# A mixture-of-experts decoder layer: the last four experts on one of two sums, and the odd tiles' statistics by accumulating passes

## The reference

```python
probs = softmax(x @ router_weight.T); topw, topi = top_k(probs, 8)
topw = topw / sum(topw)
# each expert takes its rows, at most 256 of them (CAPACITY)
gu = xe @ gate_up_proj; g, u = split(gu, 2); h = silu(g) * u
ye = h @ down_proj
y = sum over the 8 experts of a row of topw * ye
x = x + y
out = (x - mean(x)) / sqrt(var(x) + 1e-5)     # over the 512 values of a row
```

## Time and profile before

| | |
|---|---|
| median of 3 runs | 1366.23 us (1363.86 to 1369.6) |
| the profiled execution | 1370.82 us |
| its span, first to last instruction | 1368.9 us |
| mean granted TensorE clock | 0.88 |
| busy: PE, DVE, ACT, POOL | 1144.9, 1100.1, 852.6, 997.2 us |
| HBM read and written | 147.48 and 52.94 MB |

### The profile page before, as it was taken

One profiled execution on the slowest core, in us unless ns is written; L12 is line 12 of the kernel. 1 busy time (PEld: TensorE's weight loads), 2 busy tenths in 40 slices (PEclk: granted clock), 3 DMA queues, 4 the chain that ended last, 5 costly groups with the idle time before them and its releaser, 6 DMA issues. The chain is left out here.

```text
span 1368.9 us, 19497 instructions
## 1 busy us (share of the span) xinstructions
PE 1144.9 (84%) x6481; PEld 768.9 (56%) x6481; DVE 1100.1 (80%) x1534; ACT 852.6 (62%) x1536; POOL 997.2 (73%) x788
## 2 busy tenths in 40 slices
PE   7489997898968889978987536999999999999950
PEld 2234433353324544333533326999899999999950
DVE  2379988989968699778899354988889888989946
ACT  5474584734855445756354225888888888888843
POOL 0778778867999887999989703777777777777744
PEclk9688997899979689977998557999999999999985
DMA  6535326322252412163131208999999999999978
GB/s 239 136 74 193 103 64 154 108 56 72 49 139 57 129 51 64 34 152 108 31 81 32 62 17 277 267 305 303 308 301 303 307 307 307 303 314 304 302 130 331
DMA packets 97491, 235.26 MB, mean 172 GB/s; under 512 B 20705, under 2 KB 21217, under 8 KB 96753
## 3 DMA queue, kind: packets, MB, share of 16 engines
q1 hardware_dynamic: 65648, 162.66, 39.1%
q0 software_dynamic: 31744, 71.37, 21.8%
HBM read 147.48 MB, written 52.94 MB: 146 GB/s over the span
## 5 line engine op out<-in xcount | busy, mean ns | idle before, releaser
L1189 DVE TENSOR_TENSOR_SCAN hst<-hst,dbu 128x512 f32<-128x512 f32 x256 | 299.2, 1214 | 98.8 <-POOL dbu L1005 72.9
L1005 POOL TENSOR_TENSOR dbu<-rep,bc 128x1024 f32<-128x1024 f32 x128 | 301.8, 2359 | 67.1 <-PE y_ps L377 36.1
L1600 POOL DMA_INDIRECT sum_rows<-ye,tokens x128 | 205.5, 1605 | 101.0 <-ACT ye L1679 73.9
L377 PE MATMUL y_ps<-dbu,cs 128*32 128x512 f32 x512 | 158.0, 701 | 74.7 <-DVE dbu L1195 63.5
L1592 POOL DMA_INDIRECT xe<-x_rows,tokens x128 | 148.9, 1163 | 83.6 <-issue 37.8
L771 ACT ACTIVATE hst<-rep,small_sb 128x512 f32<-128x512 f32 x256 | 165.9, 685 | 47.7 <-DVE dbu L1195 42.1
L415 PE MATMUL ring<-wqkv,xT 128*128 128x512 f32 x384 | 178.7, 609 | 0.3 <-DVE x2T L1277 0.2
L1195 DVE TENSOR_TENSOR dbu<-hst,bc 128x1024 f32<-128x1024 f32 x128 | 156.7, 1225 | 4.4
L1642 PE MATMUL low<-xh,w1h 128*128 128x256 f32 x512 | 150.8, 295 | 0.7 <-DVE w1l L1753 0.7
L1642 PE MATMUL low<-xl,w1h 128*128 128x256 f32 x512 | 145.6, 284 | 0.0
L1642 PE MATMUL low<-xh,w1l 128*128 128x256 f32 x512 | 145.5, 284 | 0.0
(11 more groups left out here) (190 smaller groups left out, 2705.6 us busy)
## 6 DMA issues: line engine op xcount, KB each, us to landing
w<-in_gate_up SPq DMA_DIRECT2D x64, 768.0 KB
rep<-made SPq DMA_DIRECT2D x256, 128.0 KB
w<-in_down SPq DMA_DIRECT2D x64, 256.0 KB
bc<-bc_rows SPq DMA_DIRECT2D x64, 128.0 KB, 2.9
w<-in_down SPq DMA_DIRECT2D x64, 128.0 KB
rows<-sum_rows SPq DMA_DIRECT2D x16, 512.0 KB, 9.3
sum_rows<-x2T SPq DMA_DIRECT2D x1, 4608.0 KB, 16.7
xT<-in_x_turned SPq DMA_DIRECT2D x16, 256.0 KB, 3.0
```

The source lines that it names most:

```text
L377: ins = pe.matmul(y_ps[rows, :], sel, dbu[:, n % WORK, g, :], start=(k == 0), stop=(k == QUADS - 1))
L1005: pool.tensor_tensor(dbu[:, n % WORK, :, :], rep[:, i % 2, :, 1, :], bc[:, k, 0, :].unsqueeze(1).broadcast_to([P, 2, T]), ALU.mult).then_i ...
L1189: dve.tensor_tensor_scan(h, h, dbu[:, n % WORK, i, :], 0.0, ALU.mult, ALU.add).then_inc(scanned, 1)
L1600: pool.indirect_dma_start(sum_dram[e % SUMS], bass.IndirectOffsetOnAxis(ap=tokens[:, e, j:j + 1], axis=0), ye[:, e % YE, j, :], None, comp ...
```

## The change

The last four experts, 60 to 63, all add to the even sum (`sum_of`), so the odd sum is complete with expert 59 (`ALONE - 1`). `scatter(e)` for 61, 62 and 63 waits for the expert right before it; up to 60 it waits for e-2 as before. SP loads the whole odd sum when 59 has landed, and the whole even sum when 63 has.

In the last stage the two tiles of a pair are treated differently. For the odd tile DVE adds the sums by `scalar_tensor_tensor`, which also writes the sum over each row (`total`). ACT turns that into minus the mean and makes a Square of the tile plus this bias, with the sum over each row as a further output (`power`). For the even tile DVE does what it did for every tile. POOL copies and scales the odd tile's two numbers beside the even tile's and then works on the pair as before. ACT does `center(g + 1)` ahead of the normalization of pair g.

```diff
--- before.py
+++ after.py
@@ -1466,8 +1466,7 @@
         YE = 3
         PER = 2
         PARTS = TILES // PER
-        LOADS = ((0, 0), (0, 1), (0, 2), (1, 0), (1, 1), (0, 3), (1, 2), (0, 4), (1, 3), (0, 5), (1, 4), (0, 6), (1, 5),
-                 (0, 7), (1, 6), (1, 7))
+        ALONE = EXPERTS - 4
         tab_i = sb("tab_i", [P, P], I32)
         tab_f = sb("tab_f", [P, P])
         last_f = sb("last_f", [P, P])
@@ -1491,8 +1490,11 @@
         twice_l = sb("twice_l", [P, 2, CAP], F32R)
         ye = sb("ye", [P, YE, CJ, D])
         rows = [sb(f"rows{i}", [P, TILES, D]) for i in range(SUMS)]
-        stt = sb("stt", [P, TILES, 6])
-        mvc = sb("mvc", [P, TILES, 2])
+        stt = sb("stt", [P, PARTS, 6])
+        mvc = sb("mvc", [P, PARTS, 2])
+        total = sb("total", [P, PARTS])
+        power = sb("power", [P, PARTS])
+        square_out = sb("square_out", [P, D], F16)
         root = sb("root", [P, TILES])
         half = sb("last_half", [P, PER])
         shift = sb("shift", [P, TILES])
@@ -1533,6 +1535,9 @@
         half_set = sem("half_set")
         spread_ready = sem("spread_ready")
         var_ready = sem("var_ready")
+        total_ready = sem("total_ready")
+        centered = sem("centered")
+        power_ready = sem("power_ready")
         var_shifted = sem("var_shifted")
         root_ready = sem("root_ready")
         shift_ready = sem("shift_ready")
@@ -1549,9 +1554,18 @@
 
             return slice(0, 2 * P) if part == 0 else slice(2 * P, W1)
 
+        def sum_of(e):
+
+            return e % SUMS if e < ALONE else 0
+
+        def on_sum(i, e):
+
+            return sum(sum_of(n) == i for n in range(e + 1))
+
         def until_added(eng, e):
 
-            wait(eng, added[e % SUMS], 16 * CJ * (e // SUMS + 1) if e >= 0 else 0)
+            i = sum_of(e)
+            wait(eng, added[i], 16 * CJ * on_sum(i, e) if e >= 0 else 0)
 
         @block.sync
         def _(sp):
@@ -1573,11 +1587,12 @@
                     load_first(c + 2)
                 if has(c + 1):
                     load_second(c + 1)
-            for i, g in LOADS:
-                until_added(sp, EXPERTS - SUMS + i)
-                sp.dma_start(rows[i][:, g * PER:(g + 1) * PER, :],
-                             sum_dram[i][g * PER * P:(g + 1) * PER * P, :].rearrange("(t p) d -> p t d", p=P))\
-                    .then_inc(rows_loaded[g], 16)
+            for i, last in ((1, ALONE - 1), (0, EXPERTS - 1)):
+                until_added(sp, last)
+                for g in range(PARTS):
+                    sp.dma_start(rows[i][:, g * PER:(g + 1) * PER, :],
+                                 sum_dram[i][g * PER * P:(g + 1) * PER * P, :].rearrange("(t p) d -> p t d", p=P))\
+                        .then_inc(rows_loaded[g], 16)
             for t in range(TILES):
                 sp.wait_ge(final, t + 1)
                 sp.dma_start(out.rearrange("b (t p) d -> (b t) p d", p=P)[t], rows[0][:, t, :]).then_inc(out_stored, 16)
@@ -1594,12 +1609,12 @@
                         .then_inc(gathered[e % RAW], 16)
 
             def scatter(e):
-                until_added(pool, e - SUMS)
+                until_added(pool, e - SUMS if e <= ALONE else e - 1)
                 for j in range(CJ):
                     pool.wait_ge(ye_ready[j], e + 1)
-                    pool.indirect_dma_start(sum_dram[e % SUMS], bass.IndirectOffsetOnAxis(ap=tokens[:, e, j:j + 1], axis=0),
+                    pool.indirect_dma_start(sum_dram[sum_of(e)], bass.IndirectOffsetOnAxis(ap=tokens[:, e, j:j + 1], axis=0),
                                             ye[:, e % YE, j, :], None, compute_op=ALU.add)\
-                        .then_inc(added[e % SUMS], 16)
+                        .then_inc(added[sum_of(e)], 16)
 
             pool.wait_ge(tokens_ready, 1)
             for c in STEPS:
@@ -1607,14 +1622,18 @@
                     gather(c + 2)
                 if has(c - 3):
                     scatter(c - 3)
-            for e in range(EXPERTS - SUMS, EXPERTS):
+            for e in (ALONE - 1, EXPERTS - 1):
                 until_added(pool, e)
             pool.wait_ge(half_set, 1)
             for g in range(PARTS):
                 part = slice(g * PER, (g + 1) * PER)
-                pool.wait_ge(var_ready, PER * (g + 1))
-                pool.tensor_scalar(shift[:, part], mvc[:, part, 0], -1.0, None, ALU.mult)
-                pool.tensor_scalar(root[:, part], mvc[:, part, 1], 1.0, EPS, ALU.mult, ALU.add).then_inc(var_shifted, 1)
+                even, odd = slice(g * PER, g * PER + 1), slice(g * PER + 1, g * PER + 2)
+                pool.wait_ge(var_ready, g + 1)
+                pool.tensor_scalar(shift[:, even], mvc[:, g, 0:1], -1.0, None, ALU.mult)
+                pool.tensor_scalar(root[:, even], mvc[:, g, 1:2], 1.0, EPS, ALU.mult, ALU.add)
+                pool.wait_ge(power_ready, g + 1)
+                pool.tensor_copy(shift[:, odd], total[:, g:g + 1])
+                pool.tensor_scalar(root[:, odd], power[:, g:g + 1], 1.0 / D, EPS, ALU.mult, ALU.add).then_inc(var_shifted, 1)
                 pool.wait_ge(var_shifted, g + 1)
                 pool.tensor_tensor(root[:, part], root[:, part], half[:, 0:PER], ALU.pow).then_inc(root_ready, 1)
                 pool.wait_ge(root_ready, g + 1)
@@ -1732,10 +1751,21 @@
                     round_second(c - 1)
                 if has(c):
                     gates(c)
-            for t in range(TILES):
-                act.wait_ge(shift_ready, t // PER + 1)
-                act.activation(rows[0][:, t, :], rows[0][:, t, :], ACT.Identity, bias=shift[:, t:t + 1],
-                               scale=root[:, t:t + 1]).then_inc(final, 1)
+            def center(g):
+                act.wait_ge(total_ready, g + 1)
+                act.activation(total[:, g:g + 1], total[:, g:g + 1], ACT.Copy, scale=-1.0 / D).then_inc(centered, 1)
+                act.wait_ge(centered, g + 1)
+                act.activation(square_out[:, :], rows[0][:, PER * g + 1, :], ACT.Square, bias=total[:, g:g + 1],
+                               accum_out=power[:, g:g + 1]).then_inc(power_ready, 1)
+
+            center(0)
+            for g in range(PARTS):
+                if g + 1 < PARTS:
+                    center(g + 1)
+                act.wait_ge(shift_ready, g + 1)
+                for t in range(PER * g, PER * (g + 1)):
+                    act.activation(rows[0][:, t, :], rows[0][:, t, :], ACT.Identity, bias=shift[:, t:t + 1],
+                                   scale=root[:, t:t + 1]).then_inc(final, 1)
 
         @block.vector
         def _(dve):
@@ -1814,13 +1844,16 @@
                 if has(c):
                     gated(c)
             dve.memset(half[:, :], -0.5).then_inc(half_set, 1)
-            for t in range(TILES):
-                dve.wait_ge(rows_loaded[t // PER], 16 * SUMS)
-                dve.tensor_tensor(rows[0][:, t, :], rows[0][:, t, :], rows[1][:, t, :], ALU.add).then_inc(row_sums, 1)
-                dve.wait_ge(row_sums, t + 1)
-                dve.bn_stats(stt[:, t, :], rows[0][:, t, :]).then_inc(spread_ready, 1)
-                dve.wait_ge(spread_ready, t + 1)
-                dve.bn_aggr(mvc[:, t, :], stt[:, t, :]).then_inc(var_ready, 1)
+            for g in range(PARTS):
+                even, odd = PER * g, PER * g + 1
+                dve.wait_ge(rows_loaded[g], 16 * SUMS)
+                dve.scalar_tensor_tensor(out=rows[0][:, odd, :], in0=rows[0][:, odd, :], scalar=1.0, in1=rows[1][:, odd, :],
+                                         op0=ALU.mult, op1=ALU.add, accum_out=total[:, g:g + 1]).then_inc(total_ready, 1)
+                dve.tensor_tensor(rows[0][:, even, :], rows[0][:, even, :], rows[1][:, even, :], ALU.add).then_inc(row_sums, 1)
+                dve.wait_ge(row_sums, g + 1)
+                dve.bn_stats(stt[:, g, :], rows[0][:, even, :]).then_inc(spread_ready, 1)
+                dve.wait_ge(spread_ready, g + 1)
+                dve.bn_aggr(mvc[:, g, :], stt[:, g, :]).then_inc(var_ready, 1)
 
 
 def constants():
```

## The result

The changed kernel takes 1371.4 us (median of 11 runs, 1368.95 to 1378.63); before takes 1366.23 us (11 runs). The ratio is 1.0043, 95% interval [1.0023, 1.0062], so +5.2 us measured for +4.7 us forecast (1370.9). It lies within 0.5%, and the sign is clear.

A forecast was written before the change was run, and what follows sets the result against it. TensorE sets the pace up to expert 61's product, then the last scatters, 16 tiles on DVE and closing work. A last landing 10.15 us later and a tail 5.45 us shorter made +4.7 us, 1370.9 us; range 1364.0 to 1376.5.

The forecast's parts named there:

- row of scatters: The last experts' scatters up to the landing of the last one: it lands 10.15 us later than before.
- tail: From the landing of the last scatter to the span's end: 5.45 us shorter than before.
- step 1: Scatters of experts 61, 62 and 63 each wait for the one before to land: last landing 4.65 us later.
- step 2: Odd loads run beside the scatters of experts 60 and 61 and hold them up: last landing 5.5 us later.
- Both my bounds: Scatters held up by the odd loads: 3.1 us if they get half the time, 7.9 at an earlier trace's shares.
- The rival of unhindered scatters: Odd loads don't hold up the scatters: no change to be measured, 1363.5 to 1365.4 us; chance 0.15.
- the heavy hold-up: Loads take the engines from scatter 60 and the first half of 61: 7.9 us, median 1373.3; chance 0.26.
- Step 3: First pair of the last stage: DVE's first add 3.3 us behind SP's first even load, for 5.15 before.
- the two ends: First even load to DVE's start: 3.0 us plus 0.7 in an empty queue, or 2.95 from today's wait.
- Step 4: Last stage with the new statistics: 30.0 us for 35.45, POOL setting the pace at 2.7 us a pair.
- The doubled sum: DVE's add with a sum takes 1.22 us, 2.83 a pair, median 1373.2; chance 0.07.
- The starved loads: Odd loads don't run beside the scatters, so even loads queue behind them, up to 11 us; chance 0.02.

The follow-up runs named there:

- no_odd_loads: The changed kernel without the eight loads of the odd sum, DVE adding the even sum to itself; 1367.41 us, 0.9998 of before.
- odd_late: The changed kernel with the odd sum loaded at the end, pair by pair with the even one, once expert 63 has landed; 1.0034 of before.
- odd_after_60: The changed kernel with the odd loads held until expert 60 has landed; 1.0043 of before.
- sums_only: The changed kernel with before's statistics, so only the new sums, waits and load order; 1376.46 us, 1.0061 of before.
- lean_pool: The changed kernel with POOL's six instructions for a pair cut to four and one small instruction more on ACT; 1370.04 us, 1.0013 of before.
- last_two_lean: The changed kernel with four POOL instructions a pair and only the last two experts on the even sum; 1368.79 us, 0.9988 of before.

## Why the prediction was right, and which terms were off

The forecast was +4.7 us by +10.15 in the row of scatters and -5.45 in the tail. The profiles give +10.95 and -4.55, +6.4, and the timed runs +5.2 (interval 3.1 to 8.5, 0.23% to 0.62% of 1366.23). The two parts and their signs are as forecast. That the time came within 0.5 us is in part luck: by the profiles step 1 was 1.85 us too small, step 2 was 1.0 too large and the tail 0.9 too short, and step 2 worked in another way than I had it.

- **Step 1, the waits: 4.65 us forecast, 6.5 measured** (no_odd_loads against before, 28.3 less 21.8). The step is right and the term too small. I took 5.2 us from issue to landing and 0.05 to the next issue, a cycle of 7.06 us; it is 7.5 to 7.7 (1316.25 to 1323.97 is 7.72). Three cycles of 0.4 to 0.7 us more make most of the difference. In odd_late, with the same row, landings took 5.2 us as I had them, a cycle was 7.3 and the row 27.3, so 5.5 us. The means of the like rows (21.3 with two sums, 27.8 without loads, 32.3 for the four with loads) give 6.5 for step 1 and 4.5 for step 2, each good to about 1 us.
- **Step 2, the loads beside the scatters: 5.5 forecast, 4.5 measured** (32.75 less 28.3). The size was near, the mechanism was not. I let the loads stretch the scatters' data by a share of the engines' time: 60's in 6.1 to 10.4 us for 4.8. The data took 5.5. Of the 3.8 us that 60 paid (9.2 for 5.4), 3.1 lie ahead of its first packet: 5.2 us behind the first issue, for 2.1 in before, no_odd_loads, odd_late and odd_after_60, where no load ran at that time. sums_only and lean_pool show the same late start, 5.2 and 5.5 us. Why the first packet comes late, no run shows. 61 paid about 0.7. So the earlier trace rows, 66 to 29, and the 70 to 34 over 60's whole transfer are averages that hold stretches with packets of one queue only; they are no share at which the scatters were served. Both my bounds were built on shares, and that their middle was close is luck. The rival of unhindered scatters is out, the heavy hold-up too: it wanted 7.6 us.
- The Trainium skill ("DMA: Bandwidth & Descriptors", section on queues, rings and completion order) lets an engine go round its queues packet by packet. Where both queues had packets, 1308 to 1312 us, the trace agrees, 255 to 284. I took the rule as equal halves of the time and got a hold-up of 3.1 us; the runs show 4.5, most of it from the late first packet, which such a share doesn't contain.
- **Step 3: 3.3 us forecast, 3.7 measured** (1336.62 to 1340.30). The upper of the two ends, worked out from the loads that met an empty queue, was the better.
- **Step 4: tail 30.0 forecast, 30.9 measured,** 0.4 of it from step 3. DVE 2.13 us a pair for 2.3. POOL set the pace as forecast, at 2.58 to 2.93 us beside DVE for 2.7, and 2.01 to 2.06 behind it for 2.05. ACT was at 2.35 us a pair, where I had 2.3 to 2.7. DVE was through 17.2 us from its start for 18.4, so POOL did fewer slow pairs than I gave it, but slower ones. The doubled sum is out: 0.66 to 0.69 us for 512 columns from two fp32 sources in SBUF, no longer than the plain add beside it (0.68 to 0.72), with 0.08 us for the accumulator's read. This is against the sentence of the Trainium skill ("Vector Engine (DVE) Microarchitecture Reference", points that are easy to get wrong). No table load stands in ACT's tail.
- The starved loads are out: the odd sum was loaded by about 1319 us, long before the last landing at 1336.60. They had left when 59 had landed, as forecast, 2.2 us ahead of 60's second issue.

What the change was good for: the tail, by the statistics (-0.25% alone). What ate it: the row, by the sums (+0.61% alone), and in that row the waits more than the loads, 6.5 to 4.5 us net. odd_late shows that the early loads cost ahead of the last landing about what they save behind it.

## What to carry to other kernels

Transfers that are hidden behind others on the same 16 DMA engines are free only if nobody waits for those others; here the same edit that moved 4.2 MB ahead also put a chain of waits on the transfers beside it. Before a stream of overlapping scatters is made to go one by one, take issue to landing from the trace (5.2 to 5.5 us here, for 1.86 us between two issues) times the number of waits. Look at slices of a trace before a share is read from it: an average over a stretch in which one queue was empty for a time says nothing of how two queues share. And count the small instructions of the helper engine: two more on POOL made it the bound of a stage of eight pairs, though each lasts 0.2 us when alone.

## What the runs showed of the hardware that I had not expected

POOL's power of 128 x 2 values takes 0.73 us, but 1.21 us where it starts just behind the first of DVE's two adds (1346.82 on POOL, 1346.78 on DVE; it ends at 1348.03, with the second add). Before, with one add at a time, all eight took 0.71 to 0.73 us.

A scatter that is issued while a queue of loads runs starts late: its first packet comes 4.7 to 5.5 us behind its issue in five places (60 in after, sums_only and lean_pool, 61 in odd_after_60, 63 in last_two_lean), for 2.1 to 2.3 without loads; 61 in the first three, where the loads came to their end meanwhile, took 3.4 to 3.8. Behind that the packets of both queues go nearly one for one (255 to 284 in 1308 to 1312 us of the changed kernel).

By the time of its packets, an expert's 0.52 MB cost the DMA engines 49.1% of 8 us, 3.9 us, alone, and less beside loads: 65.6% of 4 us, 2.6, for 0.48 MB. But 61's scatters in the changed kernel, of which 0.50 MB moved in 1317.5 to 1321 us when the loads were all but over, took 78.5% of 3.5, 2.75 us. So the lower price doesn't need the loads; what makes it is open. And that 11 us of loads held the row up by only 4.5 us has another reason: 1.22 MB of them moved by 1307 and 1.60 MB in 1313 to 1317, 2.8 of 4.19 MB, while no packet of a scatter was there.

```profile
q0 software_dynamic: 275, 0.50, 78.5%
...
q1 hardware_dynamic: 830, 1.60, 105.0%
```
